# A drain of the Pool engine behind every gather and scatter of a routed-expert loop

## What is computed

```
logits = -dist2 + jnp.einsum('bld,ed->ble', x, rw) + rb
topv, topi = jax.lax.top_k(logits, TOP_K)
w = jax.nn.softmax(topv, axis=-1)
hidden = jax.nn.gelu(jnp.einsum('bld,efd->blef', x, w1) + b1, approximate=False)
exp_out = jnp.einsum('blef,edf->bled', hidden, w2) + b2
sel = jnp.take_along_axis(exp_out, topi[..., None], axis=2)
fused = jnp.sum(w[..., None] * sel, axis=2)
```

## Time and profile before

| | us |
|---|---|
| median of 3 runs | 646.68 |
| lowest and highest run | 643.97, 646.85 |
| span of the profiled execution | 694.4 |
| PE, DVE, ACT, POOL busy in it | 536.4, 364.9, 353.7, 281.1 |

### The profile page before, as it was taken

One profiled execution on the slowest core, in us unless ns is written; L12 is line 12 of the kernel. 1 busy time (PEld: TensorE's weight loads), 2 busy tenths in 40 slices (PEclk: granted clock), 3 DMA queues, 4 the chain that ended last, 5 costly groups with the idle time before them and its releaser, 6 DMA issues.

```text
span 694.4 us, 19926 instructions
## 1 busy us (share of the span) xinstructions
PE 536.4 (77%) x6242; PEld 481.6 (69%) x6242; DVE 364.9 (53%) x1325; ACT 353.7 (51%) x1079; POOL 281.1 (40%) x308
## 2 busy tenths in 40 slices
PE   4999879994502789977678789789977776679984
PEld 4967779993401489976677679678967776668942
DVE  6554779997999356545434553112334432233126
ACT  6524167775556365546445667336634434335513
POOL 4000000000451543566666743664566666645520
PEclk9999999998655799999999999999999989989998
DMA  8970000006001455444444645445866644546553
GB/s 229 255 280 9 3 3 0 0 0 243 1 1 76 120 161 157 138 131 131 131 140 143 204 124 162 135 144 146 264 207 180 183 130 133 145 122 192 174 197 122
DMA packets 55746, 92.28 MB, mean 133 GB/s; under 512 B 10352, under 2 KB 26096, under 8 KB 55152
## 3 DMA queue, kind: packets, MB, share of 16 engines
q1 hardware_dynamic: 45424, 72.35, 35.0%
q0 software_dynamic: 10240, 18.89, 9.2%
HBM read 78.07 MB, written 17.37 MB: 137 GB/s over the span
## 4 chain that ended last, share of the span: by engine, by line
PE 43%; issue 18%; DVE 18%; POOL 8%; ACT 7%; DMA 2%; DVEq 2%; another core or an unknown queue 0%; POOLq 0%; SPq 0%; ACTq 0%
PE bank L2148 15%; PE bank L2141 13%; POOL yd L600 6%; ACT value L883 3%; DVE shared L1187 2%; DVE shared L1179 2%; POOL shared L592 2%; DVE early L1467 2%; PE bank L1735 2%; DMA shared<-yd 1%; PE bank L1772 1%; PE bank L1840 1%; PE bank L1762 1%; PE bank L2133 1%; PE bank L2089 1%
## 5 line engine op out<-in xcount | busy, mean ns | idle before, releaser
L883 ACT ACTIVATE value<-bank,shared 128x128 f32<-128x128 f32 x632 | 180.8, 376 | 203.0 <-PE bank L2141 156.7
L2148 PE MATMUL bank<-shared,value 128*128 x1264 | 182.7, 290 | 62.4 <-ACT value L883 41.7
L2148 PEld LDWEIGHTS bank<-shared,value 128*128 128x128 f32 x1264 | 161.7, 200 | 76.7 <-issue 76.1
L2141 PE MATMUL bank<-early,shared 128*128 x1264 | 180.9, 288 | 5.3 <-issue 2.8
L592 POOL DMA_INDIRECT shared<-xd,early x128 | 125.5, 980 | 127.5 <-PE bank L2141 79.8
L2141 PEld LDWEIGHTS bank<-early,shared 128*128 128x128 f32 x1264 | 162.6, 200 | 9.3 <-issue 8.4
L1663 DVE SCALAR_TENSOR_TENSOR early<-bank,value,early 128x128 f32 x158 | 55.4, 351 | 195.8 <-PE bank L2148 116.6
L600 POOL DMA_INDIRECT yd<-early x128 | 128.3, 1002 | 67.8 <-DVE early L1663 36.2
L560 POOL TENSOR_TENSOR shared<-shared,xn 128x512 f32<-128x512 f32 x4 | 5.1, 1264 | 174.9 <-DVE xn L1262 167.1
L2133 PE MATMUL bank<-ident,shared 128*128 128x128 f32 x128 | 35.9, 284 | 9.0 <-DMA shared<-xd,early 5.7
L2003 PE MATMUL bank<-ksp,shared 128*128 128x32 bf16 x1536 | 40.9, 177 | 0.0
(11 more groups left out here) (334 smaller groups left out, 689.3 us busy)
## 6 DMA issues: line engine op xcount, KB each, us to landing
shared<-w1b SPq DMA_DIRECT2D x158, 258.0 KB
w1b<-in_w_t SPq DMA_DIRECT2D x1, 4096.0 KB, 17.8
shared<-col_dram SPq DMA_DIRECT2D x1, 4096.0 KB, 13.4
shared<-in_w_t SPq DMA_DIRECT2D x1, 4096.0 KB, 12.3
att<-yd SPq DMA_DIRECT2D x8, 512.0 KB
shared<-yd SPq DMA_DIRECT2D x4, 1024.0 KB, 9.1
xd<-xnT SPq DMA_DIRECT2D x2, 1280.0 KB
shared<-xd,early POOLq DMA_INDIRECT x128
```

Of the source, the lines that this page charges most:

```text
L883: ins = act.activation(hT[:, i % 2, tok(c)], bank[2 + i % 2][:, tok(c)], ACT.Gelu, bias=w1_now[:, i % WR, F + c:F + c + 1])
L2141: ins = mm(bank[2 + i % 2][:, tok(c)], w1_now[:, i % WR, tok(c)], x_now, start=True, stop=True)
L2148: ins = mm(bank[6 + i % 2][:, 0:D], hT[:, i % 2, tok(c)], w2_sb[:, bass.ds(e, 1), c, :] .rearrange("p a d -> p (a d)"), start=(c == 0), st ...
```

## The change

Each of the two functions that issue Pool's indirect transfers ends in a drain of Pool. `rows` and `results` are called 128 times each, so 256 drains are added. No wait is added or taken away, and no instruction changes its place.

```
                 pool.indirect_dma_start(out=xg[:, n % XR, :], out_offset=None, in_=xd[n // JT][:, :],
                                         in_offset=bass.IndirectOffsetOnAxis(ap=idx_src[:, n:n + 1], axis=0))\
                     .then_inc(xg_in[n % XSEM], 16)
+                pool.drain()
 
             def results(m):
                 pool.wait_ge(y_ready, step_of(m) + E)
@@
                 pool.indirect_dma_start(out=yd[:, :],
                                         out_offset=bass.IndirectOffsetOnAxis(ap=idx_dst[:, m:m + 1], axis=0),
                                         in_=yg[:, m % SLOTS, :], in_offset=None).then_inc(y_out[m % RING], 16)
+                pool.drain()
```

## The result

| | before | with the drains |
|---|---|---|
| median of the timed runs, us | 646.76 (643.97 to 647.09) | 1165.89 (1165.42 to 1169.67) |
| ratio | | 1.809, 95% interval 1.802 to 1.817 |
| span of the profiled execution, us | 694.4 | 1164.1 |
| granted clock of PE, mean | 0.923 | 0.719 |

The kernel is 519 us slower, 2.03 us for each of the 256 drains. The direction came as forecast, and so did the main mechanism, a wait for each landing.

The account below looks back on a forecast made before the run. PE was taken to bound the kernel, POOL once drained: 128 pairs at 6.0 us (flights 2.9 + 2.3, twice 0.4) make 768 us, plus 229.6 and 27.5 a span of 1025, taken as 960 us; range 860 to 1070.

Parts of the forecast that it names:

- What bounds the kernel: In the kernel before, PE at 77% busy leads; POOL keeps step with about 0.27 us to spare for each transfer.
- first rival: At POOL's drains: they wait only for POOL's own descriptor work; time 647 or about 670 us; chance 0.10.
- A drain waits for the landing: Behind each transfer, POOL's drain lasts until earlier software-made transfers have landed, 2 to 3 us from the transfer's start.
- the third: Where PE waits for gathers: short drains keep transfers apart, gathers land sooner; at most 7 us gained, 640 us; chance 0.02.
- The 6.0 us on top as a backlog: At the program's last drain: 6.0 us beyond the landing came from 256 undrained transfers, 23 ns each; absent with drains everywhere.
- The second rival: At every drain: each costs what the last one did, 8.46 us; time about 2315 us; chance 0.06.
- The rest of a cycle: On POOL between landing and next transfer: 0.19 us drain end plus 0.21 us start, 0.4 us together.
- The flights: From a transfer's start to its landing: 2.9 us for a gather, 2.3 us for a scatter.
- Every stretch POOL bound: In all stretches of POOL's list, POOL becomes the bound; pairs take 6.0 us, the 27 last scatters 73 us.
- From the sum to the time: For the whole program: the profiled span of 1025 us was converted to a timed run of 960 us.
- three ways that the forecast named: Converting span to time: shrink all by 0.931 (955 us), subtract a constant 47.7 us (977), or flights may not shrink.
- The bounds of the terms: For a gather and scatter pair: 5.04 to 7.4 us, spans 902 to 1204 us, times 840 to 1121 us.

## Why the prediction was wrong, point by point

**What bounds the kernel.** Read as "PE, with POOL in step and 0.27 us to spare for each transfer". True for the profile that was read. At 647 us, where the runs for the forecast were timed, POOL bounds the pairs by the one profile of that kind. It didn't change the forecast, since 6.0 us is beyond either, but it would have falsified the first rival's 647 us: with a drain of only 0.2 us, the pairs would have lost all of it (an estimate from the 0.30 us gaps; no run has such a drain).

**A drain waits for the landing.** Right, and read from the right row. All 256 drains end 0.07 to 0.08 us after the landing, waits in their place bring 398 of 518 us, and a drain with nothing in flight takes 41 ns. The first rival (POOL's own work only) and the third (faster) are out with it.

**The 6.0 us on top as a backlog.** Right for the change: the same last drain takes in the changed kernel

```profile
L63 POOLq DRAIN  x1: 53/53/53, 1136.8 to 1136.8; - x1
```

against 8463 ns. The second rival is out. The working, 23 ns for each transfer, was wrong.

**The rest of a cycle, 0.4 us.** This is the term that failed. It measured 0.86 us on average (0.82 in the cycle shown). The forecast took the drain's end as 0.19 us, where 0.07 were measured, and 0.21 us as the time from a wait's end to a transfer's start. That row was misread: its wait, L599, is the one of the scatter that comes next. The gather's last recorded wait is L591, and when the sequencer stood at L599 the gather was prepared already. A drain holds the sequencer itself, and 0.48 us more come behind it. The row that would have told it, 0.73 us from the gather's own wait to its start at 431.77, stood in the trace of the kernel before. 256 x 0.46 = 117 us.

**The flights.** Taken as 2.9 and 2.3 us, 5.2 a pair. They measured 2.88 and 2.49 on average, so the gather was right and the scatter too short: 128 x 0.17 = 21 us. A typical flight is shorter, 2.6 and 2.3 us by the page's medians (the lines give the KB as unknown for these transfers):

```profile
shared<-xd,early POOLq DMA_INDIRECT x128, 2.6
```

but the longest drains took 5.1 and 5.7 us, and they lift the mean. Which traffic those flights met wasn't followed. As a check, the loop took 1136.7 - 231.5 = 905 us where 768 were forecast; 117 and 21, less one rest of 0.9 since the last landing ends the loop, make these 137.

**Every stretch POOL bound.** Right, also in the middle (43.8 us expected from the last gather of the first half to the first of the second, 55.0 measured) and at the end (73 expected; 87.9 to the last start and 2.3 more). PE waits for gathers 115 times, 338 us in all. It hardly ever makes POOL wait: the longest time from a landing to the next start is 1.17 us, 0.3 above the mean.

**From the sum to the time.** The sum was 1025 us, the measured span 1164: the two terms above make 137 of the 139, and the other 2 us lie before the first gather, which came at 231.5 and not at 229.6. The forecast then took off 65 us, because the median of before was 0.931 of its span. That step was wrong too. In one and the same execution the time is 1.7 us above the span (1165.84 and 1164.1). The 47.7 us are, by the later profiles, a difference between sets of runs of the unchanged kernel, mostly in stretches in which the changed kernel waits for flights. Taking off nothing was one of the three ways that the forecast named, and the right one.

Together: 137 + 2 in the sum, 65 in the conversion, 2 between span and time: 206 us. The bounds of the terms reached to a span of 1204 us; without the deduction, and without narrowing them, 1166 would have been inside.

## What to carry to other kernels

In this kernel a drain of POOL behind an indirect transfer is a wait for the landing of what it has sent off; where transfers are issued one after another it turns a queue of flights in the air at once into one at a time. Costing such a wait takes two terms, the flight and what the sequencer could have prepared meanwhile. The second is covered up in most rows of the kernel before; look for the rare place where the sequencer itself had been held, and check by its line which instruction a wait belongs to. And when span and median of before disagree by several percent, ask first whether they come from the same execution: a ratio between two executions is not a property of profiling.

## What the runs showed of the hardware that was not expected

- A drain of POOL with nothing in flight takes 41 ns, behind a gather 2.9 us and behind a scatter 2.6 us (medians), and longer where many transfers before it had not been drained: 6.49 us with 64 of them, 4.47 with 128, 8.46 with 256. With nothing to wait for SP's and ACT's drains take 7 and 8 ns, but at the end of the program before ACT's takes 836 ns, DVE's 1259 and PE's 4075, so the 7 and 8 ns say nothing of a drain behind work. The Trainium skill, "Perfetto Trace Analysis", section "Sequencer-only Instruction (DRAIN, etc)", has a drain as the sequencer's alone; for POOL the measurements here decide otherwise.
- Between an indirect transfer's last recorded wait and the next thing POOL's sequencer does stand 0.48 us (0.53 in the one place of the kernel before). Behind a plain semaphore wait that is hidden, behind a drain it is not (0.27 and 0.86 us from a landing to the next start).
- The same unchanged kernel takes 638 to 648 us on some chips and 695 to 701 us on others (medians, each chip on one occasion). 35 of the 47 us between two such profiles lie in the stretches where a gather and a scatter go with each step (3.05 or 2.6 us a pair), beside 66 us more of idle time before PE's weight loads for `down`.
- A lone scatter's flight is the same 2.27 us at the end of both kernels, and the changed kernel moves 82 GB/s over its span where the one before moves 137: latency was paid for, not bandwidth. Both move the same bytes, 95 MB.
